# One S4/attention/Mamba/MoE tower on one core: drives as 64x64 tiles, softplus's logarithm added by TensorE, gates on two engines, exponentials ahead of masks

## What is computed

```python
h = _L0_tok_ref(A_abslog, A_phase, x, 1024)            # sums of 64 complex modes
h = h + attention(layernorm(h))                        # 16 heads, rotary, 64 tokens
h = h + layernorm(h) @ dequantize_nf4(w_idx, absmax).T + bias
h = h + mamba(layernorm(h))                            # the scan stage lies in here
h = h + base_and_lora_experts(layernorm(h))

# mamba, D = 2048 channels, N = 16 states:
delta = jax.nn.softplus(dt @ Wdt.T + dt_bias)
def step(state, xs):
    d_t, B_t, C_t, u_t = xs
    state = jnp.exp(d_t[..., None] * A) * state + (d_t * u_t)[..., None] * B_t[:, None, :]
    return state, jnp.einsum('bdn,bn->bd', state, C_t)
y = ys + u * D_param
y = y * jax.nn.silu(gate)
return y @ W_out.T
```

## Time and profile before

| | us |
|---|---|
| median of 3 runs | 4029.22 (4028.99 to 4029.43) |
| profiled execution | 4035.27 |
| span in its profile | 4033.5 |
| TensorE busy | 3869.3 (96%) |
| VectorE busy | 2690.4 (67%) |
| GpSimd busy | 2212.4 (55%) |
| ScalarE busy | 2057.1 (51%) |
| first scan of the first and of the second block | 708.1, 1653.4 |

### The profile page before, as it was taken

How to read it: one execution, slowest core, us unless ns; L and a number is a source line. 1 busy time by engine, 2 the same in 40 slices (tenths; PEclk the granted TensorE clock), 3 DMA queues, 4 the chain that set the end, 5 groups by cost and what they waited for, 6 DMA issues and landing times.

```text
span 4033.5 us, 59248 instructions
## 1 busy us (share of the span) xinstructions
PE 3869.3 (96%) x22816; PEld 2547.3 (63%) x22816; DVE 2690.4 (67%) x2934; ACT 2057.1 (51%) x3012; POOL 2212.4 (55%) x960
## 2 busy tenths in 40 slices
PE   4899999999999999999999999999999999999999
PEld 1568777444777777544577877744477877744466
DVE  6855572999446573699835555499935557289953
ACT  7842344777332344777523233677723234387732
POOL 0023433999534343799733334599943343389962
PEclk7999999999999999999999999999999999999999
DMA  4242234000322224200132223400032223410022
GB/s 114 79 145 80 86 104 159 23 16 16 118 93 86 79 84 137 98 16 16 61 114 95 79 77 117 153 13 16 26 125 94 84 84 105 160 31 16 16 89 73
DMA packets 97131, 320.23 MB, mean 79 GB/s; under 512 B 12400, under 2 KB 16752, under 8 KB 92400
## 3 DMA queue, kind: packets, MB, share of 16 engines
q1 hardware_dynamic: 80752, 275.70, 21.4%
q10 hardware_dynamic: 16128, 41.03, 3.0%
HBM read 272.51 MB, written 44.17 MB: 79 GB/s over the span
## 4 chain that ended last, share of the span: by engine, by line
PE 36%; issue 32%; DVE 20%; POOL 9%; ACT 2%; POOLq 0%; ACTq 0%; DVEq 0%
PE psg L985 22%; DVE sb_wst L1798 17%; POOL sb_wl L537 9%; PE psx L1220 5%; PE psg L1241 3%; PE psx L1293 1%; PE psg L1271 1%; DVE psg L1771 1%; DVE psg L1770 1%; PE psg L1369 1%; PE psg L1278 1%; ACT sb_yh L898 1%; PE psx L1002 0%; PE psg L1260 0%; PE psg L1195 0%
## 5 line engine op out<-in xcount | busy, mean ns | idle before, releaser
L537 POOL TENSOR_TENSOR sb_wl<-sb_raw,sb_wh 128x1024 fp32r<-128x1024 f32 x388 | 955.1, 2465 | 1740.9 <-ACT sb_wh L654 1740.6
L1798 DVE TENSOR_TENSOR_SCAN sb_wst<-sb_dA,psx 128x1024 f32<-128x1024 f32 x512 | 1130.0, 2268 | 12.3 <-PE psx L1220 10.4
L654 ACT ACTIVATE sb_wh<-sb_raw 128x1024 fp32r<-128x1024 f32 x388 | 407.4, 1053 | 544.1 <-PE psg L985 268.8
L796 ACT ACTIVATE sb_dA<-sb_dlt,sb_a_sb 128x504 f32<-128x504 f32 x1024 | 647.3, 705 | 56.0 <-DVE sb_wst L1798 53.8
L1220 PEld LDWEIGHTS psx<-sb_dgB,sb_duT 64*128 64x128 f32 x4096 | 359.9, 188 | 447.5 <-DVE sb_wst L1798 309.1
L1220 PE MATMUL psx<-sb_dgB,sb_duT 64*128 64x256 f32 x4096 | 587.5, 406 | 35.3 <-DVE sb_wst L1798 33.3
L1241 PE MATMUL psg<-sb_wst,sb_cst 64*64 64x512 f32 x4096 | 605.7, 617 | 0.9 <-ACT sb_twin L787 0.9
L572 POOL TENSOR_TENSOR sb_wst<-sb_wst,sb_cb_lo 128x1024 f32<-128x1024 f32 x256 | 600.3, 2370 | 5.0 <-DVE sb_wst L1798 5.0
L572 POOL TENSOR_TENSOR sb_wst<-sb_wst,sb_cb_hi 128x1024 f32<-128x1024 f32 x248 | 577.6, 2365 | 24.7 <-DVE sb_wst L1798 24.7
L985 PE MATMUL psg<-sb_xh,sb_wh 128*128 128x512 f32 x2080 | 535.6, 400 | 16.1 <-POOL sb_wl L537 7.1
L985 PE MATMUL psg<-sb_xh,sb_wl 128*128 128x512 f32 x2080 | 516.7, 390 | 0.0
(11 more groups left out here) (278 smaller groups left out, 4946.9 us busy)
## 6 DMA issues: line engine op xcount, KB each, us to landing
sb_raw<-in_w SPq DMA_DIRECT2D x360, 512.0 KB, 3.6
sb_raw<-w_ffn_dequantized SPq DMA_DIRECT2D x32, 512.0 KB, 3.3
gates<-sb_gt ACTq DMA_DIRECT2D x64, 256.0 KB, 2.6
sb_gin<-gates SPq DMA_DIRECT2D x64, 256.0 KB, 2.6
h_after_tok<-sb_h SPq DMA_DIRECT2D x4, 2048.0 KB, 8.7
sb_cb_lo<-c_rows ACTq DMA_DIRECT2D x8, 1024.0 KB, 6.2
sb_cb_hi<-c_rows ACTq DMA_DIRECT2D x8, 1024.0 KB, 7.5
sb_h<-h_after_tok SPq DMA_DIRECT2D x4, 2048.0 KB, 8.5
```

Source lines behind the costliest of these rows:

```text
L537: pool.tensor_tensor(rest(b, i0), raw[:, i0 % RAW, :, :], high(b, i0).bitcast(F32), ALU.subtract).then_inc(s_wl, 1)
L654: A(high(b, i0), raw[:, i0 % RAW, :, :], ACT.Copy).then_inc(s_wh, 1)
L796: ins_ = A(dA[:, (m * NQ + k) % RING, :, n, 1:S], dlt[:, m % 2, :].rearrange("p (b s) -> p b s", b=NB)[:, :, 1:S], ACT.Exp, scale=a_sb[:, ...
L1798: v.tensor_tensor_scan(wst[:, x, 4 * j:4 * j + 4, :, :].rearrange("p b n s -> p (b n s)"), dA[:, x, 4 * j:4 * j + 4, :, :].rearrange("p b ...
```

## The change

- `drives` writes its products as eight of 64 rows and 64 columns of weights each, instead of four of 64 x 128.
- `logarithm(m)` is new on TensorE: the identity times ScalarE's logarithm, added in bank 2 of `psg`. It waits for `soft_sum(m)` and the logarithm, and stands after the sums of step 2 (in the gate phase after strips 10 and 14). `drive_sum` loses its first instruction and waits for it (`s_ln`).
- Gates of even m stay on GpSimd, those of odd m go to VectorE after step 6 of the group that follows, straight from PSUM; their copies by ScalarE go. The counters are split in two (`s_y`, `s_yo`), in SP's and TensorE's waits too.
- Prelude: ScalarE takes the last sine and the exponentials before `masks(4)` (the fifth half) and its conversion of half 5; VectorE makes `masks(5)` after the coefficient arithmetic; ten halves instead of nine precede the filter groups; ScalarE makes three masks of a half from the fifth on, not from the tenth.
- In the gate phase ScalarE's `settled(1)` stands behind `decay(0, 1)`, and VectorE's `drive_sum` of m = 0 and 1 one strip later.

```diff
-EARLY = 9
-LATE = [[9], [10], [11], [12], [13], [14], [15], []]
-BY_ACT = [4 if i < EARLY else 3 for i in range(HALVES)]
+EARLY = 10
+LATE = [[10], [11], [12], [13], [14], [15], [], []]
+BY_ACT = [4 if i < 4 else 3 for i in range(HALVES)]
...
+                        if m >= 2 and m % 2 == 0:
+                            sp.wait_ge(s_y, b * (DC // 2) + m // 2)
+                        if m >= 2 and m % 2 == 1:
+                            sp.wait_ge(s_yo, b * (DC // 2) + m // 2)
...
-                            if g == 1 and m >= 2:
+                            if g == 1 and m >= 2 and m % 2 == 0:
                                 gated(m - 2)
...
-                if i + 1 < HALVES:
+                if i + 1 < HALVES and i != 4:
                     converted(i + 1)
...
-            masks(4)
             act.wait_ge(s_tab, TAB_A)
             A(gco[:, 0:2, :], gco[:, 0:2, :], ACT.Sin).then_inc(s_tabA, 1)
...
             A(gco[:, 2, :], mode[:, 0, :], ACT.Exp).then_inc(s_tabA, 1)
-            for i in range(5, EARLY):
+            converted(5)
+            for i in range(4, EARLY):
                 masks(i)
...
-                            if m >= 1:
+                            if m % 2 == 1:
                                 summed(m - 1)
...
+                    def logarithm(m):
+
+                        pe.wait_ge(s_own["sp"], b * 2 * DC + 2 * m + 2)
+                        pe.wait_ge(s_sp2, b * DC + m + 1)
+                        pe.matmul(psg[:, 2, :], C("ident"), spt[:, 0, :], start=False, stop=True,
+                                  skip_group_check=True).then_inc(s_ln, 1)
...
-                            for r in range(2):
-                                r0 = 64 * r
-                                ins_ = mm(psx[:, 2 * j + r, :].rearrange("p (a t e) -> p a t e", a=8, e=2)[:, :, :, e],
-                                          duT[r0:r0 + 64, m % 2, i * P:(i + 1) * P],
-                                          dgB[r0:r0 + 64, i, k, :, :, :], start=True, stop=True)
+                            for c in range(2):
+                                for r in range(2):
+                                    r0 = 64 * r
+                                    ins_ = mm(psx[64 * c:64 * c + 64, 2 * j + r, :].rearrange("p (a t e) -> p a t e", a=8, e=2)[:, :, :, e],
+                                              duT[r0:r0 + 64, m % 2, i * P + 64 * c:i * P + 64 * c + 64],
+                                              dgB[r0:r0 + 64, i, k, :, :, :], start=True, stop=True)
...
+                            if g == 2 and 1 <= m < DC - 1:
+                                logarithm(m + 1)
...
-            masks(5)
             v.wait_ge(s_tabA, 7)
...
+            masks(5)
             masks(6)
...
             masks(8)
+            masks(9)
...
-                        v.wait_ge(s_sp2, b * DC + m + 1)
+                        v.wait_ge(s_ln, b * DC + m + 1)
                         if m >= 1:
                             v.wait_ge(s_tr, b * DC + m)
-                        own.link(tt(x, spt[:, 0, :], x, ALU.add))
                         tt(du[:, :], x, u[:, m, :], ALU.mult).then_inc(s_dlt, 1)
...
+                            if g == 6 and m >= 2 and m % 2 == 0:
+                                gated(m - 1)
```

More of the change, by code:

```diff
@@ L351, in tower @@
         s_zr = sem("s_zr")
+        s_ln = sem("s_ln")
+        s_yo = sem("s_yo")
         s_yh, s_yl = sem("s_yh"), sem("s_yl")
@@ L864, in _ @@
                             act.preload_act_table_set(LN_EXP)
+                            decay(0, 1)
                             settled(1)
-                            decay(0, 1)
                     for m in range(DC):
@@ L1191, in delta @@
                         if m >= 3:
[L1192 removed]
+                            if m % 2 == 1:
+                                pe.wait_ge(s_yc, b * (DC // 2) + (m - 3) // 2 + 1)
+                            else:
+                                pe.wait_ge(s_yo, b * (DC // 2) + (m - 4) // 2 + 1)
                         pe.wait_ge(s_wdt[m % 2], 16 * (b * (DC // 2) + m // 2 + 1))
@@ L1321, in _ @@
                             delta(0)
+                        if m == 10:
+                            logarithm(0)
                         if m == 11:
@@ L1324, in _ @@
                             delta(1)
+                        if m == 14:
+                            logarithm(1)
                     drives(0, 0)
```

19 lines of the change are left out of this document (8 added, 11 removed).

## The result

The changed kernel takes 3982.24 us (median of four runs, 3981.32 to 3984.89), the kernel before 4029.1 us beside it: a ratio of 0.9884, 95% interval 0.9868 to 0.9899. That is 47 us, where 29.6 us were forecast. The profiled execution of after took 3982.5 us, span 3980.7 us; the one of before stood 6 us over its median, that of after stands on it.

The account below looks back on a forecast made before the run. VectorE was taken to set the 20.23 us period, two engines 0.4 us behind; -9.8 + 4.3 + 1.05 - 1.7 = -6.15 per block, -24.6 for four, and -5.0 for the prelude gave 3999.6 us, range 3990 to 4018.

Parts of the forecast that it names:

- VectorE's sum of the block: Scan stage: VectorE's logarithm sum goes from 14 groups, 0.70 us each, so 9.8 us less per block.
- Gates: Scan stage: seven odd gates move from GpSimd to VectorE, 0.61 us each, so 4.3 us more per block.
- TensorE per group: Scan stage: TensorE's work per channel group falls from 19.79 to 18.3 us with 64x64 drives and the logarithm.
- undoing the shape would give 20.8 us: Scan stage, a rival: drives keep their cost, TensorE takes 20.8 us per group and becomes the bound; 4060 us, 7%.
- The price of 62 ns per matmul: TensorE's drives: by the skill's sequencer time a drive would take 0.99 us; the prediction said the trace disagrees.
- Edges: Ends of the scan stage: cheaper drives and sums remove VectorE's waits for drives, 1.7 us less per block.
- Prelude: Before the first block: the last exponentials moved ahead and ten early halves end the prelude 5.0 us sooner.
- the ring of masks: Prelude: VectorE makes five masks per half into a ring of four, so the filters start at about 140.
- The prediction's own formula: Prelude: one half less after the filters, their later start, first filter group at full clock: 4.87 - (140 - 138.5) + 1.6 = 5.0 us.
- Between the stages: Gate phase: TensorE's logarithms of m = 0 and m = 1 add 1.05 us per block.
- The 6 us between profile and median: Whole kernel: the profiled execution, 4035.3 us, stood 6 over the median 4029.2; this difference was carried over to the forecast.

Follow-up runs that it names:

- a_link: The changed kernel with soft_sum's second operation waiting again on VectorE's own count of the first: 3989.37 us.
- a_gates_pool: The changed kernel with all gates on GpSimd, as in the kernel before: 3996.09 us.
- b_again: The kernel before, unchanged, measured and profiled once more: 4029.33 us.
- b_drives64: The kernel before with its drives as 64x64 tiles and nothing else changed: 4020.20 us.
- b_prelude: The kernel before with the whole change of the prelude and nothing of the rest: 4023.55 us.
- a_old_prelude: The changed kernel with the old prelude (exponentials behind the fifth half's masks, nine early halves, ScalarE's old shares): 3990.99 us.
- b_unlink: The kernel before with soft_sum's second operation no longer waiting on VectorE's count of the first; drive_sum waits for the second instead: 4017.14 us.
- c_spaced: The changed kernel with soft_sum's two operations set a scan apart in the scan stage, later steps moved accordingly: 3998.24 us.

## Why the prediction was right and wrong

The direction, the mechanism and all four parts held; the time fell 8 us below the range's lower end and 17.4 us below the forecast. Two steps failed, a wait put at nothing and a difference carried over as a constant. Step by step:

- **VectorE's sum of the block**, -9.8: right in kind, 0.73 instead of 0.70 us each, so -10.2. The 0.70 was read as the slot of one row; its neighbour's 0.61 stood behind a wait for it and fell to 0.58.
- **What the sum left out:** `soft_sum`'s second operation lost its wait. It is plain in the diff, and the prediction put it at nothing without a reason: it priced only operations that come or go. -1.8 per block, 7 us in all (a_link). This is the first step that failed. With it the forecast would have been 3992, inside the range but still 10 us above the measured time.
- **Gates** +4.3: measured 0.58 us, +4.1. Without them the kernel is 13.9 us slower (a_gates_pool): GpSimd would be the bound at some 19.8 us.
- **TensorE per group** 18.3: 0.86 to 0.92 us for a drive, 18.6 for the group by the starts in the changed kernel's timeline. That undoing the shape would give 20.8 us was nearly right too (20.66). The Trainium skill, page "TensorEngine Tiling (Array Packing)", section "Key Properties", says that changing the tiling mode drains TensorE; in these rows a change costs 0.16 us behind the sums and 0.20 behind a drive, and what passes inside TensorE meanwhile they do not show. The price of 62 ns per matmul that the prediction took from the Trainium skill's page "TensorE: Matmul & The Clock Gate", section "Back-to-back issue gap", does not show: 32 instructions (16 pairs) pass in 0.86 us, 54 ns for a pair.
- **Edges** -1.7: in b_again the kernel before waits 2.17 us for drives at the start of the second block and 0.78 us in the fourth, by the clock alone. A kernel whose clock stays up had less to win: b_drives64 has one stage without a low stretch, 318.38 us against 319.27 (b_prelude) for the kernel before, -0.9. About half of the 1.7 was a clock effect, taken for a fixed cost.
- **Prelude** -5.0: the filters start at 136.72 and not at 140; following the ring of masks came out 3.3 us late. The prediction's own formula with that, 4.87 - (136.72 - 138.50) + 1.6, gives 8.25, and at the end of the filters the two profiles are 231.16 - 222.65 = 8.5 us apart. But 1.6 of it is the clock at the first filter group, and the old prelude does not always lose it: in b_again this group takes 7.17 us from 137.54 on and the filters end at 228.53, in a_old_prelude at 229.60. So the new order is worth 5.9 to 7.0 us at that place. I take 6.5.
- **Between the stages** +1.05: those without a low stretch rise from 623.2 to some 624.0, +0.8. In the two profiles this is hidden by the clock's 1.3 us. Nor is the end 2.8 us shorter: before's profile has a low stretch there, and b_again comes to 165.6 us without one (after: 165.4).
- **The 6 us between profile and median** were carried over as a constant. They are not one, and this is the second step that failed. The profile of before had low stretches in every block at both places and one at its end; after's has few, and stands on its median. By stages without them, before has 319.27 and after 310.45: -8.8 each, which is -10.2 - 1.8 + 4.1 - 0.9 = -8.8.

Then 4 x (-8.8) + 4 x 0.8 - 6.5 = -38.5, and 46.9 were measured. The missing 8.4 us are of the size of the clock's part: in b_again's blocks 3 x 1.7 + 2 x 1.3 = 7.7 us, in after's 2 x 0.3 + 1.3 = 1.9, and b_again's profiled execution stood 4.6 us under its own median. No profile shows an execution of the kernel before at its median, so this last item is a size that fits and no more. The profiles show that the stretches are rarer in the changed kernel; that the change causes this is not shown, as two other small edits (b_unlink, b_drives64) also lost those ahead of the feed-forward part.

## What to carry over

Price an instruction by the distance to the next one's start, and go through a diff for waits that vanish as well as for operations. When three engines stand within 0.4 us of each other, the parts have no prices of their own: undoing one costs 6 to 65 us here, and their sum is far more than the whole. Before reading two profiles' difference as the change's, run the old kernel's profile a second time and compare stretches of equal clock.

## What was unexpected of the hardware

- A wait of VectorE for its own previous count costs 0.12 to 0.13 us, which shows between the starts and not in the durations (0.73 against 0.60 in a_link; 0.71 against 0.59 in c_spaced).
- The same work with the same pauses (TensorE 3.28, then 2.40 us busy in 4 us each) is followed by 1.2 GHz in the kernel before and by 2.4 GHz in b_unlink, at a price of 1.3 us. In one execution of one kernel (b_again) a scan stage took 321.0 us three times and then 319.25, and behind equal pauses of 1.60 us products took 0.63 us once and 0.39 once.
- A drive as eight fp32 products of 64x64 (16 instruction pairs) takes 0.86 us between 64x64 sums, 0.91 to 0.92 behind a wait or another shape, while as 64x128 it takes 1.06 us, and the sums ahead of it 1.02 instead of 0.86.
